# 1/rms through a store and a broadcast load, and node-major columns, in the first layer of a four-layer graph network

## The reference

```
x = layernorm(x + L0(x, adj))     # aggregate, dense 128->512, rms norm, silu, dense 512->128
x = layernorm(x + L1(x, adj))     # a 1x1 and a 17-tap convolution over the nodes, message passing, GRU gates
x = layernorm(x + L2(x, adj))     # three hops over the row-normalised adjacency
x = layernorm(x + L3(x, adj))     # aggregate, dense 128->256, relu, dense 256->128
```

```
agg = epsilon*x + adj @ x                         # per graph [node, 128]
h   = agg @ W1 + b1                               # [node, 512]
h   = h * rsqrt(mean(h*h over the 512) + 1e-6) * w
out = silu(h) @ W2 + b2
```

## Time and profile before

| | us |
|---|---|
| median of 3 runs (lowest, highest) | 1124.64 (1121.78, 1124.82) |
| the profiled execution's own time | 1127.47 |
| its span in the trace | 1125.6 |
| PE busy | 1072.3 |
| DVE busy | 826.1 |
| ACT busy | 715.6 |
| POOL busy | 595.5 |

### The profile page before, as it was taken

How to read it: one execution, slowest core, us unless ns; L and a number is a source line. 1 busy time by engine, 2 the same in 40 slices (tenths; PEclk the granted TensorE clock), 3 DMA queues, 4 the chain that set the end, 5 groups by cost and what they waited for, 6 DMA issues and landing times.

```text
span 1125.6 us, 24829 instructions
## 1 busy us (share of the span) xinstructions
PE 1072.3 (95%) x8013; PEld 960.3 (85%) x8013; DVE 826.1 (73%) x2548; ACT 715.6 (64%) x1335; POOL 595.5 (53%) x650
## 2 busy tenths in 40 slices
PE   7899999999999969989999999999999999999884
PEld 6799999999999958968888888888888888888774
DVE  4477777777778732634787888888888888889983
ACT  4444555455555522346777878787878787878765
POOL 1244343434334304633576666676767676766674
PEclk9999999999999969999999999999999999999988
DMA  4112332223332125862111111111111111100001
GB/s 163 55 50 85 95 92 87 87 94 95 95 94 79 55 74 163 254 199 65 58 58 48 57 57 58 57 58 58 58 57 58 58 57 58 39 29 11 20 29 38
DMA packets 64190, 84.45 MB, mean 75 GB/s; under 512 B 6464, under 2 KB 33472, under 8 KB 63808
## 3 DMA queue, kind: packets, MB, share of 16 engines
q1 hardware_dynamic: 64064, 82.86, 23.7%
HBM read 57.14 MB, written 25.69 MB: 74 GB/s over the span
## 4 chain that ended last, share of the span: by engine, by line
PE 90%; DVE 3%; issue 2%; ACT 2%; POOL 1%; DMA 1%; SPq 0%; ACTq 0%; DVEq 0%; POOLq 0%
PE banks L160 19%; PE banks L154 11%; PE banks L155 10%; PE banks L156 10%; PE banks L513 10%; PE banks L771 4%; PE banks L541 3%; PE banks L681 3%; PE banks L606 3%; PE banks L656 3%; PE banks L483 2%; PE banks L635 2%; PE banks L721 2%; PE banks L573 1%; PE banks L609 1%
## 5 line engine op out<-in xcount | busy, mean ns | idle before, releaser
L168 POOL TENSOR_TENSOR rstd<-ve,minus_half 128x4 f32<-128x4 f32 x128 | 131.5, 1027 | 72.0 <-DVE ve L1091 66.0
L168 POOL TENSOR_TENSOR r_rms<-ms,minus_half 128x4 f32<-128x4 f32 x32 | 32.3, 1008 | 224.7 <-DVE ms L1055 224.7
L513 PE MATMUL banks<-w,s 128*128 128x128 f32 x768 | 101.2, 275 | 0.4 <-DVE y L1069 0.4
L513 PEld LDWEIGHTS banks<-w,s 128*128 128x128 f32 x768 | 95.6, 192 | 3.4 <-issue 0.5
L154 PE MATMUL banks<-agg_hi,w_hi 128*128 128x512 f32 x192 | 87.5, 455 | 5.7 <-issue 5.5
L1081 DVE BATCH_NORM_STATS2 stats<-y 128x6 f32<-128x128 f32 x384 | 82.9, 279 | 1.7 <-POOL y L1443 1.5
L155 PE MATMUL banks<-agg_lo,w_hi 128*128 128x512 f32 x192 | 77.1, 402 | 0.0
L156 PE MATMUL banks<-agg_hi,w_lo 128*128 128x512 f32 x192 | 76.8, 400 | 0.0
L160 PE MATMUL banks<-at,x_rows 128*128 128x128 f32 x512 | 69.6, 280 | 3.9 <-DVE agg_lo L1043 3.0
L160 PEld LDWEIGHTS banks<-at,x_rows 128*128 128x128 f32 x512 | 65.9, 196 | 7.0 <-issue 2.3
L771 PE MATMUL banks<-w,z 128*128 128x128 f32 x512 | 68.9, 280 | 3.2 <-DVE t L1285 1.9
(11 more groups left out here) (193 smaller groups left out, 3325.4 us busy)
## 6 DMA issues: line engine op xcount, KB each, us to landing
at<-in_at SPq DMA_DIRECT2D x32, 256.0 KB, 2.9
x_rows<-in_x SPq DMA_DIRECT2D x32, 256.0 KB, 2.9
x_scratch<-x SPq DMA_DIRECT2D x32, 256.0 KB, 3.1
ad<-in_ad SPq DMA_DIRECT2D x32, 256.0 KB, 2.6
x1c<-x_scratch SPq DMA_DIRECT2D x32, 256.0 KB, 2.7
atc<-in_at SPq DMA_DIRECT2D x32, 256.0 KB, 2.9
yh<-yh_scratch SPq DMA_DIRECT2D x64, 128.0 KB, 2.8
out<-out_rows SPq DMA_DIRECT2D x32, 256.0 KB, 2.0
```

The source lines that it names most:

```text
L168: return nc.gpsimd.tensor_tensor(to[:], base[:], minus_half[:], ALU.pow)
L513: last = pe.matmul(bank[7][:, g, :], s[c][:, g, :], w2[:, c, :], start=(c == 0 and g == 0), stop=(c == H0 - 1), skip_group_check=True)
```

## The change

1/rms no longer goes through PE and ACT. `spread_rms` is gone from both. `r_rms`, 128 nodes by 4 graphs, is stored to a small tensor in memory (`store_rms`), and loaded back with every partition reading all 512 values (`load_rv`), into a ring of two `rv` tiles. The values come back in the order in which they lie in memory: nodes, then graphs. So the columns of the aggregate, of the hidden layer and of `s` are now in that order too: `neighbours` writes each graph to every fourth column of its bank, and `square_sums` and `down` load their stationary operand from every fourth column (`by_node`). The 512-column products read contiguous columns as before.

To go with this: `agg_hi` and `agg_lo` become rings of two; banks are dealt anew (the Gram product, the sums and `conv1` share bank 5); x_rows has a ring of five; the ring of `ad` has one tile instead of two, and its row sums come a turn later; stage one has one turn more; the order of the steps in the turn is new on all engines, with `hidden` split over two turns and `gram` at the end of its own turn; some start-up loads change places, w1 ahead of the table for the taps; three start-up tiles share memory with `hn`. Semaphores are merged, among them those of the stores of the first two slot pairs: the copies of pairs 6 and 7 now both wait for the stores of pairs 0 and 1.

```diff
-        X_RING, AT_RING, AD_RING, X1_RING = 4, 2, 2, 2
+        X_RING, AT_RING, AD_RING, X1_RING, RV_RING = 5, 2, 1, 2, 2
+        rms_dram = nc.dram_tensor("rms_scratch", [GROUPS, P, G], F32, kind="Internal").ap()
+        def by_node(tile):
+            return flat(tile).rearrange("p (n g) -> p g n", g=G)
...
-        TURNS1 = GROUPS + 11
+        TURNS1 = GROUPS + 12
...
             if 0 <= p < REST_PAIRS:
-                engine.wait_ge(rest_stored[p], REST_STORES)
+                engine.wait_ge(rest_stored, REST_PAIRS * REST_STORES)
...
+            def store_rms(k):
+                until(sp, "r_rms", k)
+                landed(sp, rv_in, k - 2)
+                sp.dma_start(rms_dram[k], r_rms[:]).then_inc(rms_stored[k % 2], 16)
+            def load_rv(k):
+                landed(sp, rms_stored, k)
+                until(sp, "hn2", k - RV_RING)
+                sp.dma_start(flat(rv[k % RV_RING]),
+                             rms_dram[k].rearrange("n g -> (n g)").unsqueeze(0).to_broadcast([P, G * P])
+                             ).then_inc(rv_in[k % RV_RING], 16)
...
                     stage(load_x, t + 1)
+                stage(store_rms, t - 1)
+                stage(load_rv, t - 1)
+                stage(load_ad, t + 1 - 12)
                 stage(store_x1, t - 6)
-                stage(load_ad, t + 2 - 11)
...
-                by_graph(pe, bank[6], lambda g: x_rows[k % X_RING][:, g, :],
+                by_graph(pe, by_node(bank[4]), lambda g: x_rows[k % X_RING][:, g, :],
...
-                    last = pe.matmul(bank[1][:, 0, g:g + 1], agg[:, g, :], ones[:, 0:1], start=True, stop=True)
+                    last = pe.matmul(bank[5][:, 0, g:g + 1], by_node(agg)[:, g, :], ones[:, 0:1], start=True, stop=True)
...
-            def spread_rms(k):
-                until(pe, "r_rms", k)
-                free(pe, ("hcp", k - 7), ("rv", k - 1))
-                for g in range(G):
-                    last = pe.transpose(bank[4][:, g, :], r_rms[:, g:g + 1].to_broadcast([P, P]), ident[:])
...
-                    last = pe.matmul(bank[7][:, g, :], s[c][:, g, :], w2[:, c, :], start=(c == 0 and g == 0),
+                    last = pe.matmul(bank[7][:, g, :], by_node(s[c])[:, g, :], w2[:, c, :], start=(c == 0 and g == 0),
...
             for t in range(TURNS1):                 # PE
                 stage(neighbours, t)
+                stage(down, t - 4, 3)
+                stage(hidden, t - 2, 3)
+                stage(square_sums, t - 1)
+                stage(hidden, t - 2, 2)
                 stage(conv1, t - 8)
+                stage(transform, t - 10, 1)
+                stage(down, t - 3, 0)
+                stage(hidden, t - 1, 1)
+                stage(transform, t - 10, 0)
+                stage(down, t - 3, 1)
+                stage(x1_t, t - 5)
+                stage(hidden, t - 1, 0)
                 stage(down, t - 3, 2)
+                stage(gram, t)
...
+                stage(silu, t - 3, 2)               # ACT
+                stage(silu, t - 3, 3)
                 stage(full, t)
                 stage(high, t)
-                stage(spread_rms, t - 1)
+                stage(x1_full, t - 6)
+                stage(spectrum_of, t - 10, 1)
+                stage(conv1, t - 9)
+                stage(spectrum_of, t - 10, 0)
+                stage(silu, t - 2, 1)
+                stage(silu, t - 2, 0)
...
-                until(dve, "rv", k)
+                landed(dve, rv_in, k)
...
+                stage(apply0, t - 5)                # DVE
                 stage(product, t - 1)
+                stage(normalise, t - 3, 2)
+                stage(residual0, t - 4)
                 stage(mean_square, t - 1)
+                stage(normalise, t - 2, 1)
+                stage(stats0, t - 4)
+                stage(low, t)
+                stage(normalise, t - 2, 0)
+                stage(moments, t - 4, 0, LN_EPS)
+                stage(normalise, t - 2, 3)
+                stage(row_sums, t - 12)
+                stage(conv1_bias, t - 8)
...
                 stage(add_eps, t)                   # POOL
+                stage(norm, t - 5, 0)
                 stage(x_bias, t - 3)
-                stage(norm, t - 4, 0)
                 stage(rms, t - 1)
```

More of the change, by code:

```diff
@@ L47 @@
 FIRST_STEPS = """
-ae nb agg agg_hi agg_lo gram prod sums ms r_rms spread rv hid0 hid1 hid2 hid3 hn0 hn1 hn2 hn3
+ae nb agg agg_hi agg_lo gram prod sums ms r_rms hid0 hid1 hid2 hid3 hn0 hn1 hn2 hn3
 s0 s1 s2 s3 down0 down1 down2 down xb y0 moments0 r0 x1_rows x1t x1 c1 hcp hc dft0 dft1 xh0 xh1 row_sum
@@ L192, in graph_layers @@
         ad = [rows(f"ad{i}") for i in range(AD_RING)]
-        agg, agg_hi, agg_lo = rows("agg"), rows("agg_hi", F32R), rows("agg_lo", F32R)
-        rv = rows("rv")
+        agg = rows("agg")
+        agg_hi, agg_lo = ([rows(f"agg_{n}{i}", F32R) for i in range(2)] for n in ("hi", "lo"))
+        rv = [rows(f"rv{i}") for i in range(RV_RING)]
         x1_rows = rows("x1_rows")
@@ L474, in gram @@
                 until(pe, "agg_lo", k)
-                free(pe, ("hn1", k - 1), ("prod", k - 1))
-                split_product(pe, flat(bank[0]), gram_hi[:], gram_lo[:], flat(agg_hi), flat(agg_lo),
+                free(pe, ("hcp", k - 8), ("ms", k - 1), ("prod", k - 1))
+                split_product(pe, flat(bank[5]), gram_hi[:], gram_lo[:], flat(agg_hi[k % 2]), flat(agg_lo[k % 2]),
                               True, True).then_inc(sem["gram"], 1)
@@ L523, in x1_t @@
                 for g in range(G):
-                    last = pe.transpose(bank[2][:, g, :], x1_rows[:, g, :], ident[:])
+                    last = pe.transpose(bank[1][:, g, :], x1_rows[:, g, :], ident[:])
                 last.then_inc(sem["x1t"], 1)
@@ L528, in conv1 @@
                 until(pe, "x1", k)
-                free(pe, ("rv", k + 6), ("hcp", k - 1))
-                by_graph(pe, bank[4], lambda g: x1[k % X1_RING][:, g, :], lambda g: conv1_w[:]
+                free(pe, ("ms", k + 7), ("prod", k + 7), ("hcp", k - 1))
+                by_graph(pe, bank[5], lambda g: x1[k % X1_RING][:, g, :], lambda g: conv1_w[:]
                          ).then_inc(sem["c1"], 1)
@@ L535, in transform @@
                 if half == 0:
-                    free(pe, ("hn3", k + 8), ("xh0", k - 1))
+                    free(pe, ("hn0", k + 8), ("xh0", k - 1))
                 else:
-                    free(pe, ("hn2", k + 8), ("ms", k + 8), ("xh1", k - 1))
-                psum = flat(bank[(3, 1)[half]])
+                    free(pe, ("hn1", k + 8), ("xh1", k - 1))
+                psum = flat(bank[(3, 0)[half]])
                 for i in range(2):
@@ L816, in full @@
                 until(act, "sums", k - 1)
-                copy(agg[:], bank[6][:]).then_inc(sem["agg"], 1)
+                copy(agg[:], bank[4][:]).then_inc(sem["agg"], 1)
             def high(k):
                 until(act, "nb", k)
-                until(act, "hid2", k - 1)
-                copy(agg_hi[:], bank[6][:]).then_inc(sem["agg_hi"], 1)
-            def spread_rms(k):
-                until(act, "spread", k)
-                until(act, "hn2", k - 1)
-                copy(rv[:], bank[4][:]).then_inc(sem["rv"], 1)
+                until(act, "hid2", k - 2)
+                until(act, "gram", k - 2)
+                copy(agg_hi[k % 2][:], bank[4][:]).then_inc(sem["agg_hi"], 1)
             def silu(k, c):
@@ L1048, in product @@
                 until(dve, "agg", k)
-                V.scalar_tensor_tensor(out=agg[:], in0=bank[0][:], scalar=gram_c[:], in1=agg[:], op0=ALU.add,
+                V.scalar_tensor_tensor(out=agg[:], in0=bank[5][:], scalar=gram_c[:], in1=agg[:], op0=ALU.add,
                                        op1=ALU.mult).then_inc(sem["prod"], 1)
@@ L1054, in mean_square @@
                 until(dve, "r_rms", k - 1)
-                V.tensor_scalar(ms[:], bank[1][:, 0, 0:G], sum_b[:], RMS_EPS, ALU.add, ALU.max
+                V.tensor_scalar(ms[:], bank[5][:, 0, 0:G], sum_b[:], RMS_EPS, ALU.add, ALU.max
                                 ).then_inc(sem["ms"], 1)
@@ L1100, in conv1_bias @@
                 until(dve, "hc", k - 1)
-                V.tensor_tensor(hcp[:], bank[4][:], over_graphs(conv1_b), ALU.add).then_inc(sem["hcp"], 1)
+                V.tensor_tensor(hcp[:], bank[5][:], over_graphs(conv1_b), ALU.add).then_inc(sem["hcp"], 1)
             def row_sums(k):
@@ L1352, in rms @@
                 until(pool, "ms", k)
-                until(pool, "spread", k - 1)
+                landed(pool, rms_stored, k - 1)
                 powers(ms, r_rms).then_inc(sem["r_rms"], 1)
```

97 lines of the change are left out of this document (34 added, 63 removed).

## The result

The changed kernel takes 1273.98 us (1271.20 to 1275.90, 4 runs), the kernel before 1124.16 (1121.78 to 1124.82, 4 runs): 1.1335 times as long, 95% interval 1.1308 to 1.1363. The forecast was 1114, so it is wrong by 160 us and on the wrong side. The second rival, a weight load with a step of 16 bytes at half rate, gave 1256.

A forecast was written before the change was run, and what follows sets the result against it. PE was taken to bound the kernel, busy throughout a stage-one turn. Terms -14.1 - 1.0 + 3.2 + 1.0 gave -10.9 us, so 1114 us, own range 1105 to 1122, full range 1105 to 1150.

The forecast's parts named there:

- The second rival: PE's weight loads with a step of 16 bytes run at half rate: 1256 us in all, chance 0.17.
- I take 0 for both: Stage one's 40 strided loads a turn and the strided PSUM writes of `neighbours` were both priced at no extra time.
- the upper bound: High end for the 40 strided loads a turn: 0.22 us each instead of 0.111, 142 us in all.
- The second argument: PE's float32 load already goes at a slow 0.87 ns a column, supporting a stride surcharge of 0.
- Transposes, and the order (-14.1): PE in stage one: dropped transposes save 0.44 us in each of 32 groups; the new order costs 0; turn 11.12 us.
- The write of neighbours (0): Strided PSUM writes in stage one cost 0: a pass of 0.058 us can double under a load of 0.111.
- the third rival: Only the strided PSUM write is slow, four times, and the load isn't: 1145 us, chance 0.08.
- The path of 1/rms: Store lands in 2.1 us, load in 2.9; `rv` is ready 4.7 us before DVE wants it, so no cost.
- Ramp and drain (-1): Filling and emptying stage one's pipe together gain 1 us, between -4 and +3; the drain keeps a cycle of about 5.5 us.
- The handover (+3.2): Into stage two: late row sums delay SP's stores and ACT's copy of pair 6, stalling PE 3.2 us; bounds 0 to 8.
- The hand-offs (+1): Banks in stage one's new turn are freed only 0.1 to 0.3 us before needed: 1 us in all, up to 9.
- the first rival: Strides cost little, but another engine's order, at bank 5, keeps the turn at 11.56 us: about 1127 us, chance 0.13.

The follow-up runs named there:

- e_silu_writes: Changed kernel with ACT's silu writing `s` by graphs in 512-byte steps and `agg` reordered from PSUM, so PE loads contiguously: 1115.49 us, 0.9914 of the kernel before.
- e_gmajor: Changed kernel with columns kept graph by graph and the store of 1/rms writing 512 single floats instead: 1209.83 us, 1.0767 of the kernel before.
- e_hand: `e_silu_writes` with POOL's wait moved behind its negations and separate semaphores for the stores of pairs 0 and 1: 1112.41 us, 0.9891 of the kernel before.

## Why the prediction was wrong, step by step

**The failed step** is "I take 0 for both" under the strided loads and writes. For the loads the surcharge was 0.122 us each: four pieces of `down` (3 x 0.97 + 0.85) and one of sums (0.85) make 4.6 us a turn. The turns of `e_silu_writes` and of the changed kernel, 11.20 and 15.72, differ by 4.52. 32 times that is 144.6; with the 15.8 of the clock it is 160.4, and stage one of the two kernels differs by 159.7. So the loss of stage one has these two parts, and no room for a third of size. (From the kernel before it is less, 139.5, because the terms below that gained are in it.)

The rate that I took as the upper bound was nearly right by chance: I had it from loads at half clock (0.22), and the stride makes 0.233 at the full clock. What failed was the choice between the bounds. I chose by ACT's copy of the transform, which reads PSUM with steps of 544 bytes at no cost. That reading was true, and strided reads of PSUM stayed cheap in the runs (582 to 628 ns against 598; 751 against 751). But it says nothing of a reader of SBUF. The same copy also writes `xh` in SBUF, in pairs of neighbouring floats 512 bytes apart: two floats to a 16-byte line, which by the table above is nearly free for a load too. It never tested one float to a line, the case of `by_node`. Where ACT does walk SBUF in steps, it pays: silu of 512 floats goes from 717 to 1205 or 1221 ns. That is 0.95 to 0.98 ns a float on top. If the silu's own price is the 0.83 ns a column of a copy, which no run shows, it is 1.78 to 1.81 ns a float, near PE's 1.82 per line. For ACT, then, the memory was the variable: the same step of 16 bytes cost about 0.5 us a piece on reading SBUF and at most 0.03 us on reading PSUM. The prediction itself had said "another reader and another memory" and then priced the doubt at 0.17.

The second argument, that a load of 0.87 ns a column is slow and so has room, failed too. That room exists: a line at 1.82 ns costs nothing until half a line per float, and step 2 is nearly free by it. It was just too small for step 4. (The sentence that the load is 85% of PE's time misreads: PEld is busy for 85% of the span, 90% of PE's busy time.)

The Trainium skill had the rule against the change (Advanced Engine Details and Errata, Memory Cachelines): at least two hits on each 16-byte line in SBUF, else a penalty. The trace agrees, with its number: two floats to a line 0.94 for eight loads, one float to a line 1.86. Its other half, that a PSUM pattern that isn't contiguous slows matmuls significantly, no run here shows: `neighbours` writes in steps of 16 bytes at 0.89 per eight, the price of a contiguous group of four in the earlier trace rows. But by the prediction's own bound a pass of 0.058 us could double there behind its load without being seen.

**Transposes, and the order (-14.1).** Right in its mechanism. 11.125 us a turn was predicted with free strides, `e_silu_writes` has 11.20. From the 11.565 of the earlier trace rows that is 32 x 0.365 = 11.7 us off.

**The write of neighbours (0).** Right in its price: nothing of it shows in the turn, and with that the third rival is out.

**The path of 1/rms.** Right. In the changed kernel the store lands in 1.4 us (2.1 taken) and the load in 4.0 (2.9 taken): 5.4 against the 5.2 of the estimate with its issue. DVE waited for `rv` for 0.8 us in all. `e_gmajor` shows that the cover of some 5 us is a real bound: forecast trip and cover together are 9.9 us, the trip of 15 is 5 over, and turns grow by 1.4 to 3.9 us.

**Ramp and drain (-1).** Too small. With PE's loads contiguous, stage one gained 20.2 us, of which the turns are 11.7, so 8.5 are ramp and drain. The last group enters (`add_eps`) at 344.9 us instead of 359.8, 14.9 earlier, so 3 to 4 of the 8.5 lie ahead of the drain and stay unexplained. In the drain, the granted clock was 0.82 on average before and `hcp` came every 5.5 us while it was low; now the clock is 1.00 in the same stretch, and `hcp` comes every 3.7 to 3.9 us, in the changed kernel and in `e_silu_writes`:

```profile
392.70 0.69 DVE L1112 TENSOR_TENSOR hcp<-banks,conv_b 128x512 f32<-128x512 f32 x1
...
396.55 0.69 DVE L1112 TENSOR_TENSOR hcp<-banks,conv_b 128x512 f32<-128x512 f32 x1
```

I had taken the cycle of 5.5 us as fixed by its dependences, while part of it was the low clock: the kernel before has one at full clock as well, from 420.37 to 424.10 us, of 3.73. Why the clock stays up in the new drain is not shown; PE has more work in those turns.

**The handover (+3.2).** The row sums came 3.2 to 3.5 us apart, as predicted (3.35), and SP started 10.0 us behind stage two where 8.0 was forecast: the sum of group 28 stood at 566.21, behind its own load, 1.9 us later against stage two than the place behind `hcp` that I gave it. But POOL also waits in `everything_first`, between its fifth and its sixth negation for PE's slots; that wait, in the code and overlooked, held PE for 4.95 us, and the clock afterwards was 0.53 for some six microseconds. Stage two lost 7.9. It hid the stall that I had predicted, and no run shows that one by itself. `e_hand` takes POOL's wait away, but the merged semaphore with it, so pair 6 is free there and 2.7 us appear on pair 7. Its stores land at 435.49, 28.4 us behind the start of stage two, where the forecast had 27.1; with the semaphore still merged that would be a stall of about 4.4 us at pair 14 (an estimate: 435.49 and 0.60 for the copy, against 407.1 + 24.6 for PE by the earlier trace rows).

**The hand-offs (+1), the first rival.** The 0.075 a turn between 11.125 and 11.20 make 2.4 us, over the 1 taken and inside the 9 allowed. Bank 5 never set the turn: PE has no wait in the full turns of either kernel.

**The sum.** -10.9 was forecast for free strides; `e_silu_writes`, where PE loads nothing with a stride, is at -10.1 by the medians and -12.5 by the spans. This agreement is partly luck: ramp and drain gave 7.5 more than taken, stage two took 4.5 more (7.7 for 3.2), the turns gave 1.4 less than their two terms together (11.7 for 13.1). The second rival was right in its mechanism, and its 1256 is under the 1274 by about the clock, which the prediction did not price. The range, 1105 to 1150, had no price for the case that held, and 0.17 was too small a chance for a bound of 142 us that rested on a row.

## What to carry to other kernels

Before a tile is laid out so that one engine reads it with a stride, count the 16-byte lines per element for each reader of SBUF, and give the stride to the engine with idle time: here the same permutation cost PE 145 us, and ACT 0.49 us a silu, none of which shows in the time. Evidence from one memory did not carry to the other, so bound an unseen access by rows of the same memory, or not at all. When work is moved to the end of a stage, look up every engine that waits for the last of it, not only the one whose path was traced.

## What the runs showed of the hardware that was not expected

- A float32 weight load of 128 columns costs 0.111 us at step 1 and 0.117 at step 2, and then grows with the 16-byte lines touched to 0.233 at step 4 and 0.237 at step 8. ACT pays 0.95 to 0.98 ns a float more in SBUF, for a read in steps of 16 bytes or a write in steps of 512.
- Strides in PSUM cost nothing that shows for PE's writes (0.89 per eight loads, which bind there) and DVE's reads (751 ns), and within 5% for ACT's reads.
- 512 floats stored one by one land in 8.5 to 11.9 us, taken to the issue of the load that waits for them, the same 2 KB in runs of 16 bytes in 1.4.
- In a steady stream that never waits, the granted clock fell to the 1.2 GHz level for about three microseconds in ten of twenty turns, each time behind the eight sums, whose matmuls move a single column, where `down` and the sums both read one float in four. With a step of eight in `down` it was rarer (four of twenty turns; 0.95 to 1.00 over stretches of 100 us), with a step of three one turn had it, with a step of two or one none, nor with the sums contiguous. It costs 1.6 us each time. What sets it off was not settled.
